# Second cross attention: six score banks in named pairs, two for the rest, and a new order of the frame's pieces

## What is computed

```
def _L1_xattn_ref(query, key, value, Wq, Wk, Wv, Wo, bo):
    B, T, D = (2, 512, 256)
    H = 16
    HD = D // H
    b, t, d = query.shape
    ...
    q = split_heads(query @ Wq.T)
    k = split_heads(key @ Wk.T)
    v = split_heads(value @ Wv.T)
    q = _apply_rope(q)
    k = _apply_rope(k)
    scale = 1.0 / jnp.sqrt(jnp.asarray(HD, dtype=q.dtype))
    logits = jnp.einsum('bhqd,bhkd->bhqk', q, k) * scale
    attn = jax.nn.softmax(logits, axis=-1)
    out = jnp.einsum('bhqk,bhkd->bhqd', attn, v)
    out = out.transpose(0, 2, 1, 3).reshape(b, t, d)
    return out @ Wo.T + bo
x = x + _L1_xattn_ref(_layernorm(x, axis=-1), ctx_1024, ctx_1024, L1_xattn_Wq, L1_xattn_Wk, L1_xattn_Wv, L1_xattn_Wo, L1_xattn_bo)
```

## Time and profile before

| | |
|---|---|
| median of three runs | 3267.02 us (3264.29 to 3269.05) |
| the profiled execution: time, span | 3263.24 us, 3261.3 us |
| granted clock of PE, mean | 0.945 |
| busy of the span: PE, DVE, ACT, POOL | 88%, 72%, 51%, 29% |
| the stage of the change, about | 1739 to 2470 us of the span |

### The profile page before, as it was taken

How to read it: one execution, slowest core, us unless ns; L and a number is a source line. 1 busy time by engine, 2 the same in 40 slices (tenths; PEclk the granted TensorE clock), 3 DMA queues, 4 the chain that set the end, 5 groups by cost and what they waited for, 6 DMA issues and landing times. The chain is left out here.

```text
span 3261.3 us, 76408 instructions
## 1 busy us (share of the span) xinstructions
PE 2857.9 (88%) x28240; PEld 2046.7 (63%) x28240; DVE 2332.5 (72%) x5011; ACT 1675.1 (51%) x3314; POOL 959.9 (29%) x1223
## 2 busy tenths in 40 slices
PE   7998999999999996749997999999987989846881
PEld 6886566666666664637884666666656777734661
DVE  5998567777777775558886666666654999965667
ACT  4776555655555553325552444444435878833440
POOL 0000344555555554430001000000001244455551
PEclk9999999999999997879998999999988999968995
DMA  7930444555455552450001333333314777865557
GB/s 175 292 87 4 136 139 133 161 161 150 139 143 160 161 152 73 142 177 10 0 0 41 69 68 67 66 65 68 68 32 139 219 222 229 231 184 147 163 154 247
DMA packets 364785, 413.70 MB, mean 127 GB/s; under 512 B 108016, under 2 KB 330512, under 8 KB 364368
## 3 DMA queue, kind: packets, MB, share of 16 engines
q1 hardware_dynamic: 218176, 220.63, 25.6%
q10 hardware_dynamic: 127216, 139.94, 15.5%
q0 software_dynamic: 19104, 49.22, 4.5%
HBM read 125.33 MB, written 252.45 MB: 116 GB/s over the span
## 5 line engine op out<-in xcount | busy, mean ns | idle before, releaser
L2167 DVE TENSOR_REDUCE x_top<-x_scores 112x2 f32<-112x750 f32 x256 | 231.2, 935 | 116.3 <-PE x_scores L2025 111.7
L812 POOL TENSOR_TENSOR x_rstd<-x_var,g_minus_half 112x1 f32<-112x1 f32 x128 | 75.0, 586 | 728.5 <-DVE x_var L808 727.9
L1367 ACT ACTIVATE x_probs<-x_held,x_minus_top 112x488 f32<-112x488 f32 x256 | 177.7, 697 | 173.6 <-DVE x_minus_top L1423 173.6
L1240 POOL TENSOR_TENSOR x_probs<-x_probs,x_inverse 112x488 f32<-112x488 f32 x256 | 250.7, 1000 | 10.2
L1281 PE MATMUL x_ring<-w_xkv,x_kv 128*122 128x512 f32 x512 | 236.3, 594 | 0.0
L1274 PE MATMUL x_ring<-x_kv,w_xkv 128*128 128x488 f32 x512 | 233.1, 588 | 1.1 <-ACT x_kv L1343 1.1
L930 ACT ACTIVATE x_v<-x_ring 122x512 f32<-122x512 f32 (+1 forms) x224 | 113.0, 504 | 176.9 <-PE x_ring L1281 151.7
L1417 DVE SCALAR_TENSOR_TENSOR x_held<-x_scores,x_keep 112x976 f32<-112x976 f32 x128 | 150.4, 1175 | 74.1 <-PE x_scores L1294 51.9
L2133 ACT ACTIVATE x_probsT<-x_scores 125x1792 f32<-125x1792 f32 x96 | 159.8, 1665 | 77.6 <-PE x_scores L2044 77.6
L812 POOL TENSOR_TENSOR a_rstd<-a_var,g_minus_half 112x1 f32<-112x1 f32 x64 | 35.7, 558 | 536.9 <-DVE a_var L808 536.9
L2025 PE MATMUL x_scores<-x_slots 32*112 32x375 f32 x1024 | 170.2, 535 | 26.0 <-DVE x_top L2167 14.1
(11 more groups left out here) (484 smaller groups left out, 7553.5 us busy)
## 6 DMA issues: line engine op xcount, KB each, us to landing
expert_slots<-d_empty ACTq DMA_DIRECT2D x32, 3612.0 KB, 17.6
by_position<-r_by_position SPq DMA_DIRECT2D x64, 784.0 KB
first_slots<-d_empty SPq DMA_DIRECT2D x8, 3612.0 KB, 34.7
r_bias<-by_position SPq DMA_DIRECT2D x64, 392.0 KB
m_rows<-expert_slots SPq DMA_DIRECT2D x143, 129.0 KB
x_kq_swapped<-x_kq_raw ACTq DMA_DIRECT2D x64, 243.5 KB
x_slots<-x_kq SPq DMA_DIRECT2D x512, 30.4 KB
m_rows<-expert_replies SPq DMA_DIRECT2D x32, 448.0 KB, 8.5
```

Source lines behind the costliest of these rows:

```text
L1240: self.nc.gpsimd.tensor_tensor(probs, probs, self.inverse[0:T, u:u + 1].to_broadcast([T, XK]), ALU.mult).then_inc(self.weighted, 1)
L1367: nc.scalar.activation(self.probs[u % 6][0:T, :], self.held[m % 2][0:T, i, :], ACT.Exp, scale=self.scale, bias=self.minus_top[0:T, m % 2, ...
L2167: nc.vector.tensor_reduce(self.top[0:T, g, 2 * half:2 * half + 2], self.scores[0:T, 1024 * half:1024 * (half + 1)].rearrange("t (a c) -> t ...
```

## The change

Three things change together, all in `ContextAttention` (the two lines in `stream` only make the number of score banks a setting).

1. The score tile grows from four banks to six, in three pairs 0, 1 and 2. Each `g` or `h` has a pair by name (`first_pair`), each `tr` two neighbouring pairs. The ring shrinks from four banks to two.
2. The list has a new order. The ages are the same.
3. `bank_free` no longer has waits by hand: it looks back through the list for the last user of each pair and waits for that one's maximum or exponential. The swap transfers and the write of `top_wide` now follow whichever piece comes last in the list.

```
-        self.plan = Flow(4, [("g0", 3), ("h0", 3), ("headsB", 5), ("g1", 3), ("h1", 3), ("k0", 1), ("stats", 0),
...
+        self.plan = Flow(2, [("h0", 3), ("g0", 3), ("headsB", 5), ("tr0", 4), ("g1", 3), ("q", 1), ("back0", 5),
...
+        self.first_pair = {"g0": 0, "g1": 0, "g2": 2, "g3": 1, "h0": 1, "h1": 0, "h2": 2, "h3": 0,
+                           "tr0": 1, "tr1": 0, "tr2": 0}
+        names = [name for name in self.plan.names if name in self.first_pair]
+        self.score_names = names
+        self.last_maximum = [name for name in names if name[0] in "gh"][-1]
+        self.last_raw = [name for name in self.plan.names if name in ("q", "k0", "k1")][-1]
...
+    def exchange(self, act, name, b):
+        if name == self.last_raw:
+            self.ready_all(act, ("q", "k0", "k1"), b)
+            for i in range(2):
+                act.dma_start(self.kq_swapped[64 * i:64 * (i + 1), :, :],
+                              self.kq_raw[64 * (1 - i):64 * (2 - i), :, :]).then_inc(self.swapped, 16)
+
+    def pairs_of(self, name):
+        first = self.first_pair[name]
+        return {first, first + 1} if name[0] == "t" else {first}
+
     def bank_free(self, pe, name, b):
...
-        if name[0] in "gh":
-            g = int(name[1])
-            at_least(pe, self.maxed["gh".index(name[0])], b * HG + g)
-            at_least(pe, self.exped, (b - 1) * CC + (2 if g > 1 else 0))
-        else:
-            i = int(name[2])
-            at_least(pe, self.exped, b * CC + i)
-            n = (b + 1) * HG + (HG if i == 2 else 2)
-            for half in range(2):
-                pe.wait_ge(self.maxed[half], min(n, self.NB * HG) if isinstance(b, int) else n)
+        names, age = self.score_names, self.plan.age
+        here = names.index(name)
+        waits = {}
+        for pair in self.pairs_of(name):
+            for back in range(1, 2 * len(names)):
+                frame, at = divmod(here - back, len(names))
+                other = names[at]
+                if pair not in self.pairs_of(other):
+                    continue
+                before = b + (age[name] - age[other] + frame)
...
+                i = int(other[-1])
+                sem, per = (self.exped, CC) if other[0] == "t" else (self.maxed["gh".index(other[0])], HG)
+                waits[other] = (sem, before * per + i + 1)
+                break
+        for sem, count in waits.values():
+            pe.wait_ge(sem, count)
```

More of the change, by code:

```diff
@@ L1917 @@
     scale = HD ** -0.5
+    score_banks = 6
     def __init__(self, nc, G, W):
         super().__init__(nc, G, W)
-        self.plan = Flow(4, [("g0", 3), ("h0", 3), ("headsB", 5), ("g1", 3), ("h1", 3), ("k0", 1), ("stats", 0),
[3 rows of a table removed]
-                             ("headsA", 4)],
+        self.plan = Flow(2, [("h0", 3), ("g0", 3), ("headsB", 5), ("tr0", 4), ("g1", 3), ("q", 1), ("back0", 5),
[3 rows of a table added]
+                             ("project", 5), ("put", 3)],
                          bankless=("tr0", "tr1", "tr2", "g0", "h0", "g1", "h1", "g2", "h2", "g3", "h3", "rope", "stats", "scale"),
                          ahead=8, behind=5, turns=3, unroll=12)
+        self.first_pair = {"g0": 0, "g1": 0, "g2": 2, "g3": 1, "h0": 1, "h1": 0, "h2": 2, "h3": 0,
[4 more added lines that the diff above has]
+        self.last_raw = [name for name in self.plan.names if name in ("q", "k0", "k1")][-1]
     def allocate(self, sb, sem):
@@ L2018, in pe @@
             g, half = int(name[1]), "gh".index(name[0])
-            if name == "g0":
+            if name == self.score_names[[n[0] in "gh" for n in self.score_names].index(True)]:
                 pe.wait_ge(self.slotted, 256 * (b + 1))
@@ L2024, in pe @@
                 slot = slice(SLOT * a, SLOT * (a + 1))
-                ins = nc.tensor.matmul(self.scores[0:T, 512 * a:512 * a + S2], slots[slot, g, S2:KQ], slots[slot, g, 0:S2],
+                at = 512 * (2 * self.first_pair[name] + a % 2)
+                ins = nc.tensor.matmul(self.scores[0:T, at:at + S2], slots[slot, g, S2:KQ], slots[slot, g, 0:S2],
                                        start=True, stop=True)
@@ L2043, in pe @@
                     slot = slice(SLOT * a, SLOT * (a + 1))
-                    ins = nc.tensor.matmul(self.scores[0:CK, 512 * a + g * T:512 * a + (g + 1) * T],
+                    at = 512 * (2 * self.first_pair[name] + a) + g * T
+                    ins = nc.tensor.matmul(self.scores[0:CK, at:at + T],
                                            slots[slot, g, i * CK:(i + 1) * CK], self.q[slot, g, :], start=True, stop=True)
@@ L2113, in act @@
             self.copy_out(act, c, body, self.kq_raw[:, :, S2:KQ], lambda bank: bank[:, 0:DC * T].rearrange("p (g t) -> p g t", g=DC))
+            self.exchange(act, name, b)
         elif name in ("k0", "k1"):
-            if name == "k0":
-                at_least(act, self.turned, b)
+            at_least(act, self.turned, b)
             self.copy_out(act, c, body, self.kq_raw[:, int(name[1]), 0:S2], lambda bank: bank[:, 0:S2])
[L2118 to L2123, removed]
+            self.exchange(act, name, b)
         elif name in ("v0", "v1", "v2"):
```

13 lines of the change are left out of this document (9 added, 4 removed), and 6 rows, old and new, of tables (scale, score_banks).

## The result

The changed kernel takes 3249.51 us (median of 17 runs, 3239.97 to 3257.62) against 3267.52 us for the kernel before on the same chip (17 runs, 3254.20 to 3277.45). The ratio is 0.9948, 95% interval 0.9938 to 0.9958. It is faster by about 17 us, where 38 were forecast.

A forecast was written before the change was run, and what follows sets the result against it. PE was taken to set the pace in the steady part (busy 578.2 of 589.8 us). Gains 26 + 9 + 1 + 2 = 38 took the profiled 3263.2 to 3225; with 3.8 for the median, 3229 us; range 3213 to 3256.

The forecast's parts named there:

- The fill: Filling frames at the stage's start: idle time, part of it behind maxima, would shrink; gain 2 us (-1 to 5).
- rival 3: The ring of two is too small: copies behind exponentials on ACT stall PE 2.3 us a frame; 3289 us, chance 0.08.
- The drain: Three draining frames after the steady ones: 53.3 us at full clock against 65.3; gain 9 us (5 to 12).
- The allowance for the clock: Three draining frames: 3 us taken off the gain of 12, as PE will idle at 0.80 of the clock.
- The last 23 us: End of the stage: three exponentials in a chain in both kernels; gain 1 us (-1 to 3).
- The steady part: 26 full frames: each falls from 20.89 to 19.9 us, 1.0 less; gain 26 us.
- the hitch at the loop's turn: Where the loop turns back among the 26 frames: 5.8 us lost, forecast to stay.
- three-piece block: h2, g3 and h3 in the new steady frame: g3 and h3 run abreast, 1.64 us in all.
- the change of tile shape: PE switching tile shape between pieces: no visible price, nothing added for 14 changes a frame against 17.
- rival 1: h2, g3 and h3 run in order, 2.46 us instead of 1.64; gain 17 us, 3250 us, chance 0.10.
- ctx0: In the steady frame ctx0 waits for the copy out of onT's bank on ACT, late by 0.1 us.
- Rival 2: DVE bounds the steady frame's second half: swap lands 1 us later, put late by 0.9; 3252 us, chance 0.12.

The follow-up runs named there:

- second pair of profiles: The changed kernel and the kernel before, each run and profiled once more without edits; ratios 0.994 and 1.0004 to the kernel before.
- run 1: Changed kernel's new order with four score banks and a ring of four; ratio 1.0655 to the kernel before.
- run 2: Old order of the kernel before with six score banks in pairs and a ring of two; ratio 1.0041 to the kernel before.
- run 3: Changed kernel with DVE doing rope after top_wide in the eight written-out frames; ratio 0.9946 to the kernel before.
- run 9: Changed kernel with g1 behind q, k1, k0 in the first scores frame, and v2 and g0 repeated in the fill; ratio 0.9915 to the kernel before.
- run 7: Changed kernel with v2 (three, then five times) and g0 (four times) repeated in two filling frames; ratio 0.992 to the kernel before.

## Why the prediction was off

**The fill was the step that failed.** "Fill: 6.4 us idle between 1770 and 1812, part of it behind maxima: 2" looked for waits that would go, and never laid out the new order for the frames in which most pieces are missing. It measured -7.5, and -8.8 in the second pair of profiles. What the runs put in its place:

- The ring of two, at the start: 2.7 us up to the first score product (33.0 instead of 30.4, and of 29.0 when the kernel before was run again). With the ring of four it comes at 30.8 in the new order too (run 1), with the ring of two at 32.1 in the old order (run 2). rope of element 0 ends 15.4 us into the stage with ring of four and old order, 15.7 with ring of four and new order, 17.5 and 18.4 with a ring of two. The rule that I set beside rival 3, the Trainium skill's (Perfetto Trace Analysis, Matmuls) that groups should rotate through different PSUM banks so that copies overlap the next products, bears on this: with only two banks to rotate through, the copies show as waits here and in run 2 (1.0 a frame), but not in the steady frames of the changed kernel. DVE's first swapped operation, which answers to the earlier trace rows, comes at 16.0 instead of 13.1 us:

```profile
1762.20 1.17 DVE L2210 TENSOR_TENSOR x_kq<-x_kq_swapped,g_constants 128x974 f32<-128x974 f32 x1 [3.07 <-DMA x_kq_swapped<-x_kq_raw]
```

- The first frame with scores, up to the first put: 5.2 us. rope ahead of the last maxima makes put wait for `top_wide`; with rope behind them (run 3) this part is 2.2 shorter, though the part behind put then loses 1.4 of it. What is left in run 3 are waits that the kernel before has shorter or not at all: 1.8 for copies out of the ring and 2.8 of g1 for g0's maximum, where it has 1.7 for a maximum there. With g1 moved and the clock held (run 9) this part is 0.9 shorter. No run removes all of these at once, so the split of the 5.2 is read from the traces and not shown.
- Behind the first put nothing was lost, but nothing gained either: the granted clock there is 0.87 where it was 0.96 before, and with it kept up this part is 3.6 us shorter (run 9).

**The drain** was mis-sized. At full clock I had 53.3, and with the clock kept up it measured 54.2; frame by frame 19.5, 17.4 and 16.4 against 18.5, 18.6 and 17.0. The allowance for the clock, 3 us because "PE will idle as it does now, at 0.80 of the clock", was right only in the best profiles: the three frames took 56.4 to 60.0, so 2 to 6 above 54.2, and 59.8 in the one that the table uses. **The last 23 us** lost 2.6 instead of gaining 1. From tr2 of the last element to its `project` it takes 14.4 us where it took 10.4. `project` of the element before and its addition now stand between headsA and headsB, and headsB waits for the bank:

```profile
2444.75 1.97 PE L2095 MATMUL x_ring<-x_probsT,x_v 125*32 125x112 f32 x48 [0.59 <-DVE g_residual L1587]
```

The last part took 22.1 with the new order and the ring of four (run 1) and 21.7 with the old order and the ring of two (run 2), 25.9 in the changed kernel, and 22.5 to 27.7 over the seven profiles with its drain. No run was made for it, and its cause stays open.

**The steady part held.** Frame 19.9 forecast, 19.66 measured, with 20.2 to 20.7 in five; 28.4 for 26, and 25 to 29 over all profiles. In part two misses cancel: at 1.23 a frame the 26 would gain 32, of which the longer frames took back some 4, and the hitch at the loop's turn shrank by 0.8. The 0.24 a frame that were not summed come from pieces that were shorter, g1 (0.73 for 0.82), the three-piece block (1.45 for 1.64) and tr0 (0.97 for 1.07), less small amounts the other way. That last one bears on the change of tile shape: the prediction found no price by comparing h3 ahead of xT with g0 and h0 ahead of headsB, but both of these change the shape. tr0 ahead of g1 keeps the 32 rows and takes 0.97, tr1 and tr2 ahead of other shapes 1.07. So a price of up to 0.1 is possible; no run tells it from quarters that are free early. The three-piece block ran abreast (1.45; rival 1 out), tr0 and tr1 made no wait that the trace shows, and ctx0 waited 0.15 to 0.3 in a few frames. **Rival 2** came in small: the swap, at 4.17 from issue to use, left put just in time, as laid out, and about every sixth landing was 0.4 to 1.0 late. It cost some 4 us in all, not 23. **Rival 3** did not happen in the steady frames; waits for the ring of two, up to 1.4 each, show in the fill.

The median fell by 18.0 where the stage fell by 23.7 in the first pair of profiles. With the stage of the kernel before at 725.8 in its second profile, and a ratio known to 3 us, the two do not disagree.

## What to carry to other kernels

Price a new order of a software pipeline three times: in the steady frame, in each filling frame and in each draining one, each laid out with the pieces that are missing. Here the steady frames gave 28.4 us where 26 were forecast, and the edges took 4.7 where I had counted on a gain of 12. Where PE's waits grow only a little, look up whether the clock held behind them; in one drain frame, filling two waits of 2.3 us in all with repeated products gave back 3. It gave back nothing in the fill while two waits there were left uncovered. And test banks and order apart: here each alone made the kernel slower.

## What the hardware showed

- In run 7 PE's granted clock stood at 0.50 (1.2 GHz) behind g1's wait of 1.39, and again behind a single wait of 1.08, although PE had been busy for 6.0 of the 6.5 us ahead of that one. The Trainium skill (TensorE: Matmul & The Clock Gate, A second HAM failure mode: psum-queue depth-cycling) tells of frequent short idle times between groups of products with which the clock swings between its two levels; the traces agree in kind, but here one short wait was enough.
- The same waits do not always do it. In the second drain frame waits of 0.89 and 1.41 stand in both profiles of the changed kernel, and it took 21.25 us at a clock of 0.84 in one and 18.60 at 1.00 in the other. Such scatter, 3 us, is as large as some terms of the sum.

```profile
2385.30:2406.55 21.25, 18.00 (x251) 11.72 (x250) 10.93 (x18) 7.11 (x9) 0.00 (x0) 0.84 0.16 25
```

```profile
2361.15:2379.75 18.60, 15.32 (x251) 10.10 (x250) 10.95 (x18) 7.10 (x9) 0.00 (x0) 1.00 0.19 29
```

- The swap needs 4.2 us from issue to use, whether ACT's queue issues both transfers or SP's one of them.
